# A fused Mamba-style mixer between two MoE layers: ScalarE, not GpSimd, makes the mixer's bias tiles

## The reference, cut to what matters

```
u = x @ W_in + b_in                      # 256 -> 512 channels
u = causal depthwise conv(u, 4 taps) + conv_b
h[t] = tanh(A) h[t-1] + u[t] * Bp        # 16 states for every channel
y[t] = Cp . h[t] + Dp * u[t]
out = silu(y) @ W_out + b_out
```

## Time and profile before

| | us |
|---|---|
| median of 3 runs (866.89 to 869.25) | 868.56 |
| the profiled execution, its own time | 869.6 |
| its span | 867.8 |
| TensorE busy | 827.1 (95%) |
| VectorE busy | 484.1 (56%) |
| GpSimd busy | 466.7 (54%) |
| ScalarE busy | 390.6 (45%) |

### The profile page before, as it was taken

The page is one execution under the profiler, slowest core; times in us unless marked ns, Lnnn a source line. Parts: engine busy times, 40 slices in busy tenths (PEclk is TensorE's granted clock), DMA queues, the critical chain, the costliest instruction groups (busy, mean ns, idle before and its releaser), DMA issues.

```text
span 867.8 us, 16211 instructions
## 1 busy us (share of the span) xinstructions
PE 827.1 (95%) x5302; PEld 719.2 (83%) x5303; DVE 484.1 (56%) x979; ACT 390.6 (45%) x766; POOL 466.7 (54%) x444
## 2 busy tenths in 40 slices
PE   4999999999999999999999999999999999999993
PEld 3778988888888878888888888888788888888883
DVE  7788853333333336768998986777333333333452
ACT  4643334343343434557687776233343343434330
POOL 6528870333334068849999982786332233230785
PEclk9999999999999999999999999999999999999998
DMA  9963553555554246210010015255354555521665
GB/s 307 326 254 104 176 170 122 195 191 206 180 212 151 81 93 115 37 25 13 21 43 25 25 51 194 73 170 171 128 169 159 193 200 199 188 66 37 130 140 149
DMA packets 53158, 119.07 MB, mean 137 GB/s; under 512 B 6443, under 2 KB 41397, under 8 KB 48757
## 3 DMA queue, kind: packets, MB, share of 16 engines
q0 software_dynamic: 17776, 75.25, 27.8%
q1 hardware_dynamic: 34834, 43.15, 15.2%
q10 hardware_dynamic: 498, 0.02, 0.0%
HBM read 83.25 MB, written 35.14 MB: 136 GB/s over the span
## 4 chain that ended last, share of the span: by engine, by line
PE 73%; POOL 13%; DVE 5%; issue 4%; DMA 3%; ACT 0%; POOLq 0%; DVEq 0%; SPq 0%; ACTq 0%
PE bank L424 21%; PE bank L426 21%; PE bank L425 21%; POOL acc L1929 4%; PE bank L629 4%; DVE v L1541 2%; PE bank L598 2%; DMA wr_hi<-w_routed 2%; POOL xs_sorted L1855 2%; PE bank L491 2%; POOL wr_lo L1899 2%; POOL yr L2046 1%; POOL v L1827 1%; PE bank L502 1%; POOL hT_lo L1831 1%
## 5 line engine op out<-in xcount | busy, mean ns | idle before, releaser
L1899 POOL TENSOR_TENSOR wr_lo<-wr_raw,wr_hi 128x3072 fp32r<-128x3072 f32 x14 | 95.4, 6816 | 96.9 <-DMA wr_hi<-w_routed 88.6
L424 PE MATMUL bank<-wr_hi,xT_hi 128*128 x312 | 130.2, 417 | 1.0 <-POOL wr_lo L1899 1.0
L1929 POOL DMA_INDIRECT acc<-ys_sorted,pos x52 | 86.2, 1658 | 81.0 <-issue 51.4
L1206 DVE TENSOR_TENSOR hT_lo<-bank,hT_hi 128x512 fp32r<-128x512 f32 x78 | 53.9, 691 | 124.7 <-ACT hT_hi L881 124.7
L426 PE MATMUL bank<-wr_lo,xT_hi 128*128 x312 | 123.4, 396 | 0.0
L1499 DVE TENSOR_TENSOR hf<-sg,bank 128x512 f32<-128x512 f32 x78 | 53.6, 687 | 124.4 <-PE bank L426 124.4
L425 PE MATMUL bank<-wr_hi,xT_lo 128*128 x312 | 122.9, 394 | 0.0
L424 PE MATMUL bank<-xT_hi,ws_hi 128*128 128x512 f32 x256 | 102.6, 401 | 2.2 <-DVE xT_lo L1206 2.2
L425 PE MATMUL bank<-xT_hi,ws_lo 128*128 128x512 f32 x256 | 100.9, 394 | 0.0
L426 PE MATMUL bank<-xT_lo,ws_hi 128*128 128x512 f32 x256 | 100.7, 393 | 0.0
L908 ACT ACTIVATE sg<-bank 128x512 f32<-128x512 f32 x64 | 38.2, 597 | 130.5 <-PE bank L426 112.8
(11 more groups left out here) (248 smaller groups left out, 2163.2 us busy)
## 6 DMA issues: line engine op xcount, KB each, us to landing
wr_raw<-w_routed POOLq DMA_DIRECT2D x16, 1536.0 KB, 7.2
wr_hi<-w_routed POOLq DMA_DIRECT2D x16, 1536.0 KB
rows<-xs_sorted SPq DMA_DIRECT2D x78, 128.0 KB, 2.3
ys_sorted<-rows SPq DMA_DIRECT2D x78, 128.0 KB
xg<-xT_kept SPq DMA_DIRECT2D x12, 512.0 KB
xT_kept<-xTf SPq DMA_DIRECT2D x9, 512.0 KB, 2.6
acc<-x SPq DMA_DIRECT2D x8, 512.0 KB, 9.9
xs_sorted<-zeros POOLq DMA_DIRECT2D x4, 1024.0 KB, 8.4
```

The costliest lines, as they stand in the source:

```text
L424: pe.matmul(o, a_hi, b_hi, start=start, stop=False, skip_group_check=True)
L1206: return dve.tensor_tensor(o, full, f32(h), ALU.subtract)
L1899: pool.tensor_tensor(wr_lo[:, e % 2, :], wr_raw[:, :], f32(wr_hi[:, e % 2, :]), ALU.subtract).then_inc(s_wl, 1)
L1929: pool.indirect_dma_start(out=acc[:, tt, :], out_offset=None, in_=ys_dram, in_offset=bass.IndirectOffsetOnAxis(ap=pos[:, tt:tt + 1], axis= ...
```

## The change

conv_bias moves from GpSimd to ScalarE. On GpSimd it was a tensor_scalar (times conv_b, plus 0.0); on ScalarE it is an activation Copy with a scale for each partition. Before the loop it stands behind ln2_hi(1), in the loop behind state_hi(n+1, 0) and ahead of ln2_apply(n+2). Its waits (s_vb, and s_step for the first) and the semaphore s_cbs, which edge_bias and add_bias wait for, are the same.

```diff
@@ scalar
+            def conv_bias(i):
+                for cb in range(CB):
+                    if i > 0:
+                        act.wait_ge(s_vb, 4 * (2 * i - 1) + cb + 1)
+                    act.activation(cbs[:, cb, :], step[:, i, :], ACT.Copy, scale=vec[:, cb, 4:5]).then_inc(s_cbs, 1)
@@ attention, before the loop
                 ln2_hi(1)
+                act.wait_ge(s_step, 16)
+                conv_bias(0)
@@ attention, in the loop
                         state_hi(n + 1, 0)
+                    if n >= 2 and n % 2 == 0:
+                        conv_bias(n // 2)
                     if live(n + 2):
                         ln2_apply(n + 2)
@@ gpsimd
-            def conv_bias(i):
-                for cb in range(CB):
-                    if i > 0:
-                        pool.wait_ge(s_vb, 4 * (2 * i - 1) + cb + 1)
-                    pool.tensor_scalar(cbs[:, cb, :], step[:, i, :], vec[:, cb, 4:5], 0.0, ALU.mult,
-                                       ALU.add).then_inc(s_cbs, 1)
@@ before the loop
             gather(NH + 1, s_ga[NH + 1])
-            pool.wait_ge(s_step, 16)
-            conv_bias(0)
             ln2_rsqrt(2)
@@ in the loop
                 if live(n) and n >= 2:
-                    if n % 2 == 0:
-                        conv_bias(n // 2)
                     edge_bias(n)
```

## The result

The changed kernel takes 869.14 us in the median of 20 runs (867.91 to 872.14), the one before 867.68 (866.29 to 869.43): the medians are 1.5 us apart. The ratio of all their runs is 1.0019, interval 1.0012 to 1.0026, or 1.6 us more. The prediction was 0.6 us less, so it had the wrong sign. In a second comparison the ratio was 1.0013 (1.0004 to 1.0023).

A forecast was written before the change was run, and what follows sets the result against it. TensorE was taken to wait in the mixer for taps held up by GpSimd's queue. Of 1.35 us earned by iteration 5, some 0.75 go back, leaving 0.6 us: 868.0 us forecast, range 865.8 to 870.1.

The forecast's parts named there:

- What bounds the kernel: Mixer: TensorE and GpSimd neck and neck; late taps hang on GpSimd's queue, 2.0 us of TensorE's tap waits within reach.
- The price of the copies: ScalarE: 0.52 us a copy, four landed after 2.18 us, GpSimd going on some 0.04 us after.
- Iteration 2: Mixer loop: last step of edge_bias on GpSimd at 417.96 against 418.46, 0.5 us earlier.
- iteration 4: Mixer loop: last step of edge_bias at 454.77 against 456.22, 1.45 us earlier; TensorE then 1.35 us early in iteration 5.
- Iteration 6: Mixer loop: last step of edge_bias at 490.65 against 490.03, 0.6 us later, eating into GpSimd's 1.19 us idle.
- the second rival: Mixer: copies of 0.69 us without overlap, iteration 6 2.1 us late, 0.9 us lost: 869.5 us; chance 0.22.
- The rigid shift: Mixer sum: TensorE's earlier times were subtracted unchanged from later instructions, such as 1.35 us from state_hi in iteration 6.
- the 1.35 us earned: TensorE's lead in iteration 5, 0.5 + 0.85 us, of which some 0.75 were to be given back in iterations 6 and 7.
- The first set: Group 0, before the loop: tap copy up to 0.1 us late, or 0.8 by the upper bound; cost and gain nothing.
- D: Experiments' theory: the change ties GpSimd's queue to TensorE through state_hi, so a late TensorE in iteration 1 costs time.
- the forecast proper: Whole kernel: median 868.0 us; 0 to 1.3 us faster, chance 0.5.

The follow-up runs named there:

- e7: Kernel before with the three bias-tile sets in the loop left out, the first pair's tiles serving all groups: mixer 145.17 us, ratio 0.9977.
- e5: Changed kernel with the loop's bias-tile copies one place earlier on ScalarE, ahead of state_hi(n+1, 0): mixer 144.93 us, ratio to the kernel before 0.9975.
- e8: Changed kernel with the scale left out of the sixteen copies: four copies 2.18 us, mixer 147.20 us; total not comparable.
- e14: Kernel before, unchanged, profiled again; it got a long half-clock stretch in iteration 1: mixer 146.23 us, edge_bias of iteration 2 at 50.18 us.

## Why the prediction was wrong, by its own steps

**What bounds the kernel** was right: TensorE's tap waits hang on GpSimd's queue, and e7 and e5 recover them. The price was not: 1.5 to 1.8 us are to be had, not 2.2, as xl is next late.

**The price of the copies** failed first, as a term of the sum. The sum took 0.52 us each from a copy without a scale and the handover from GpSimd to ScalarE, 0.04. Measured: 2.55 us for four, not 2.18, and 417.91 - (415.19 + 2.55) = 0.17 us from ScalarE to GpSimd. That is 0.50 us a set. I had the row that says otherwise: the scaled copy's successor came 0.57 us later, and I put the difference down to PSUM. e8 puts the scale at 0.09 us, more than that difference, so that by these rows the copy from PSUM is the cheaper one, 0.57 against 0.61. The budget of the Trainium skill (ScalarE: Activation LUTs, Rules for kernel authors), by estimate 2.9 us for the four, was too high: the next instruction follows 2.46 us after the first starts.

**Iteration 2** was to gain 0.5 and gained nothing; **iteration 4** was to gain 1.45 and gained 0.44, which is 1.45 less twice 0.50. So TensorE was 0.44 us early in iteration 5, not 1.35.

**Iteration 6** was to be 0.6 us late and was 2.02: 0.6 + 0.9 for TensorE's smaller lead + 0.5. That is past the 1.19 us which the prediction named as the point where the second rival decides. Its price there was 0.9; the undisturbed mixer measures 0.57. So the second rival, given 0.22, is what happened, by its path and nearly by its terms: it had 2.80 us from the first copy to GpSimd, and 2.72 were measured. But the copies do overlap, at 0.61 us each and not 0.69; the handover makes up for it.

**The rigid shift** failed too, as e8 shows: at 0.52 us a copy, the forecast's own price, the gain does not come (147.20 us, against 147.27 with the scale). "Of the 1.35 us earned" presumes that TensorE keeps its lead to iteration 6; in e8 the lead brings xl and y_low together in the other order, and 0.82 us are gone. The sum moved all instructions rigidly and never asked what meets what.

**The first set** was right: ScalarE's first tap copy is 0.4 us late and nothing comes of it, and GpSimd's 3.8 us go into idle time (9.6 us rather than 5.74).

**Not foreseen at all** was D, a wait put at nothing. The prediction noted that edge_bias now waits for ScalarE, which waits for TensorE, and took this only at the times of one trace. It is also a new dependence: before, GpSimd came to its tiles in iteration 2 without a wait for ScalarE even when TensorE was late in iteration 1 (e14). With a long half-clock stretch this wait adds 1.0 us to the changed kernel's mixer (148.27 against 147.27) and none to that of the kernel before. The measured time lay inside the stated range, whose upper end came from the second rival; the forecast proper, 0 to 1.3 us faster, had half of the chances and did not come.

## What to carry to other kernels

Where work is moved to an idle engine, its place in that engine's queue decides: behind an instruction that waits for the bounding engine it is late by that wait; ahead of that instruction it fills the same wait, here at no cost while TensorE was on time. Neither place is free of the bounding engine's lateness, as long as anything ahead of it in the queue waits for that engine: a long half-clock stretch cost the one place 1.0 us and the other 1.24. Ask of each new wait not only what it costs at the times of the trace, but what it couples that was independent. And a gain of under a microsecond in a chain of a few nanoseconds' margins is no forecast: shift the neighbours by it and see who meets whom.

## What the runs showed of the hardware

A per-partition scale makes a ScalarE copy of 128x512 from SBUF to SBUF cost 0.61 us of queue rather than 0.52. VectorE's 128x1024 subtraction and GpSimd's 128x512 one, both with two inputs in SBUF, get in each other's way: 10 ns in their start decide which takes 1.1 us more. Around the same wait of TensorE (2.12 us in all 18 profiles), the same code was granted the full clock throughout in eight profiles and the lower level for 2 to 8 us in ten; the kernel before and the changed one both had it in some profiles and not in others.
